# Stacking attention operands through a DRAM scratch in a fused attention and quantised-FFN kernel

## What is computed

```python
def attn(x, Wq, Wk, Wv, Wo):
    q = (x @ Wq).reshape(B, S, 16, 32).transpose(0, 2, 1, 3)
    k, v = (repeated 4 times over heads from (x @ Wk), (x @ Wv))
    scores = einsum('bhqd,bhkd->bhqk', q, k) / sqrt(32)
    out = einsum('bhqk,bhkd->bhqd', softmax(scores), v)
    return merge_heads(out) @ Wo
def ffn(x, weight, bias):
    w_q, w_scale = int8 rounding of weight by its row maximum / 127
    x_q, x_scale = int8 rounding of x by its token maximum / 127
    return (x_q @ w_q.T) * x_scale * w_scale + bias
x = layernorm(x + attn(x, ...)); x = layernorm(x + ffn(x, ...))
```

## Time and profile before

| | |
|---|---|
| median of 3 runs | 786.63 us (784.62 to 788.5) |
| profiled execution | 787.02 us, span 785.2 us |
| PE busy | 735.6 us (94%) |
| DVE, ACT, POOL busy | 615.2, 477.5, 596.8 us |
| chain that ended last, shares | PE 45%, POOL 16%, issue 15%, SP's queue 10% |
| of it SP's stacking issues, line 312 | 9% |

### The profile page before, as it was taken

One profiled execution on the slowest core, in us unless ns is written; L12 is line 12 of the kernel. 1 busy time (PEld: TensorE's weight loads), 2 busy tenths in 40 slices (PEclk: granted clock), 3 DMA queues, 4 the chain that ended last, 5 costly groups with the idle time before them and its releaser, 6 DMA issues.

```text
span 785.2 us, 12326 instructions
## 1 busy us (share of the span) xinstructions
PE 735.6 (94%) x3700; PEld 433.8 (55%) x3700; DVE 615.2 (78%) x1090; ACT 477.5 (61%) x872; POOL 596.8 (76%) x705
## 2 busy tenths in 40 slices
PE   8789989899899999999999999999999999999993
PEld 6455545566366654566446663666545664454451
DVE  3797888668987788886888789878888868888546
ACT  3165556556765576656666566656756666666735
POOL 4258858676997689885987779975998759898935
PEclk9799999999999999999999999999999999999997
DMA  7632223133231342223322332413422233022121
GB/s 213 175 95 55 56 58 96 52 91 101 67 111 46 101 100 91 69 72 91 95 80 71 95 101 63 122 41 94 108 84 68 76 93 102 28 56 67 51 47 54
DMA packets 56386, 65.57 MB, mean 84 GB/s; under 512 B 25665, under 2 KB 27713, under 8 KB 56321
## 3 DMA queue, kind: packets, MB, share of 16 engines
q1 hardware_dynamic: 55152, 61.91, 29.5%
q0 software_dynamic: 1168, 2.89, 1.5%
HBM read 20.71 MB, written 8.39 MB: 37 GB/s over the span
## 4 chain that ended last, share of the span: by engine, by line
PE 45%; POOL 16%; issue 15%; SPq 10%; ACT 4%; DVE 4%; DMA 3%; POOLq 3%; DVEq 0%; ACTq 0%
POOL prob_sum L1080 14%; PE front_bank L341 9%; SPq L312 9%; PE st_bank L416 8%; PE s_bank L385 7%; PE o_bank L433 7%; PE tail_bank L341 6%; PE z_bank L459 3%; POOLq L1089 2%; DVE row_max L865 2%; ACT probs L695 1%; PE front_bank L348 1%; PE tail_bank L529 1%; DMA xq_sb<-round_sb 1%; POOL x_tok L1098 1%
## 5 line engine op out<-in xcount | busy, mean ns | idle before, releaser
L865 DVE TENSOR_REDUCE row_max<-s_bank 128x1 f32<-128x512 f32 x496 | 329.1, 682 | 81.2 <-PE s_bank L385 78.4
L695 ACT ACTIVATE probs<-st_bank 128x512 f32<-128x512 f32 x512 | 290.4, 594 | 133.1 <-PE st_bank L416 114.5
L1080 POOL TENSOR_TENSOR prob_sum<-prob_sum,probs 128x512 f32<-128x512 f32 x248 | 310.6, 1285 | 8.1 <-ACT probs L695 8.1
L416 PE MATMUL st_bank<-q_stack,k_stack 98*128 98x512 f32 x512 | 224.6, 441 | 14.6 <-ACT probs L695 11.1
L385 PE MATMUL s_bank<-k_stack,q_stack 96*128 96x512 f32 x496 | 203.4, 412 | 8.3 <-DVE row_max L865 7.1
L1080 POOL TENSOR_TENSOR prob_sum<-probs 128x512 f32<-128x512 f32 x128 | 161.3, 1284 | 46.0 <-PE z_bank L459 23.9
L416 PEld LDWEIGHTS st_bank<-q_stack,k_stack 98*128 98x128 f32 x512 | 96.1, 188 | 104.8 <-ACT probs L695 55.0
L433 PE MATMUL o_bank<-probs,v_tok 128*32 128x512 f32 x1024 | 123.3, 598 | 0.1
L385 PEld LDWEIGHTS s_bank<-k_stack,q_stack 96*128 96x128 f32 x496 | 94.2, 190 | 40.2 <-DVE row_max L865 22.5
L1085 POOL TENSOR_TENSOR rs<-mv,small 128x1 f32<-128x1 f32 x64 | 12.2, 190 | 82.1 <-DVE mv L915 81.5
L433 PEld LDWEIGHTS o_bank<-probs,v_tok 128*32 128x32 f32 x1024 | 26.7, 109 | 59.4 <-issue 52.5
(11 more groups left out here) (199 smaller groups left out, 992.8 us busy)
## 6 DMA issues: line engine op xcount, KB each, us to landing
q_stack<-q_parts SPq DMA_DIRECT2D x348, 64.0 KB, 2.0
x_tok<-in_L_attn_x SPq DMA_DIRECT2D x36, 256.0 KB, 3.0
y_sb<-in_L_attn_x SPq DMA_DIRECT2D x28, 256.0 KB, 2.8
out<-z_sb SPq DMA_DIRECT2D x28, 256.0 KB, 2.1
k_stack<-k_parts SPq DMA_DIRECT2D x84, 64.0 KB, 2.0
probs<-in_L_attn_Wq SPq DMA_DIRECT2D x1, 1024.0 KB, 7.6
prob_sum<-in_L_attn_Wo POOLq DMA_DIRECT2D x4, 256.0 KB, 4.3
q_stack<-neg_max SPq DMA_DIRECT2D x64, 8.0 KB, 1.8
```

What stands on the lines that cost most here:

```text
L416: nc.tensor.matmul(st_bank[:, j % 2, :], k_stack[0:STACK_M, p, j, kt * P:(kt + 1) * P], q_stack[0:STACK_M, i, j, :], start=True, stop=True ...
L695: nc.scalar.activation(probs[:, kt, j, :], st_bank[:, j % 2, :], ACT.Exp, scale=SCALE).then_inc(exp_done, 1)
L865: nc.vector.tensor_reduce(row_max[:, i % 2, j * QT + qt:j * QT + qt + 1], s_bank[:, qt % 2, :], AX_X, ALU.max).then_inc(max_done, 1)
L1080: nc.gpsimd.tensor_tensor(prob_sum[:, j, :], first, probs[:, kt, j, :], ALU.add).then_inc(sum_done, 1)
```

## The change

A job is no longer copied by twelve DMAs inside the on-chip memory. `spill` writes its 128 by 2 by 512 parts in one DMA to a scratch in DRAM (`q_spill`, `k_spill`), and `fill` reads it back in three, one for each third of the stack, 32 partitions with four runs of 2 KB each. `fill` waits for the write's semaphore and for the last reader of the slot, and has its own place in SP's queue (`fill_sp`). ACT waits for the write alone before it reuses `q_parts` or `k_parts`. K and Q0 of batch 0 (SP and POOL) and Q2 of batch 0 (POOL) still go by twelve DMAs.

In the prologue Q1's second part follows the second pair of scores instead of the first, V's twelve passes stand behind pairs 2 to 7, two each, and VT behind the first part of Q2; `wkv_part(1)` on DVE moves ahead of Q0's split and `wq_part(2)` one pair forward. `diagonal_scales` moves from DVE to ACT. POOL's trial run of `pow` is preceded by a multiply and an add. All three tables have new places; of `MIDDLE` those of the front, SP and the second layer's first half are shown.

```diff
-FIRST_ORDER = (0, 1, 2, 3, K, Q0, Q1, Q2, V, VT, Q3)
+FIRST_ORDER = (0, 1, 2, 3, K, Q0, Q1, V, VT, Q2, Q3)
-FIRST_V_PE, FIRST_V_ACT, FIRST_VT = (0, 1, 2), 2, 3
+FIRST_V_AFTER = range(2, 8)
 MIDDLE = dict(
-    front_pe={Q3: (0, 1, 3, 4), 0: (5,), 1: (10,), 2: (13,), 3: (16,), K: (18, 22), Q0: (23, 24, 25, 27), V: (29, 30), VT: (33,), Q1: (36, 37), Q2: (44, 45)},
-    front_act={Q3: 3, 0: 5, 1: 10, 2: 13, 3: 16, K: 22, Q0: 27, V: 29, VT: 32, Q1: 38, Q2: 45},
-    front_dve={Q3: 4, 0: 6, 1: 11, 2: 15, 3: 16, K: 22, Q0: 27, Q1: 39, Q2: 45},
+    front_pe={Q3: (0, 1, 2), 0: (5,), 1: (10,), 2: (13,), 3: (17,), K: (18, 22), Q0: (23, 25, 26, 27), V: (29, 30), VT: (31,), Q1: (35, 36, 38), Q2: (44, 45)},
+    front_act={Q3: 4, 0: 6, 1: 10, 2: 12, 3: 16, K: 21, Q0: 26, V: 30, VT: 33, Q1: 37, Q2: 45},
+    front_dve={Q3: 4, 0: 6, 1: 11, 2: 14, 3: 16, K: 22, Q0: 27, Q1: 39, Q2: 47},
+    fill_sp={Q3: 10, K: 30, Q0: 28, Q1: 42, Q2: 48},
...
-    max_lo_dve=(11, 26, 45, 59),
+    max_lo_dve=(12, 27, 45, 59),
...
-    round_act=(21, 31, 39, 47),
-    unround_act=(22, 31, 43, 52),
-    turn_sp=(21, 29, 42, 49),
+    round_act=(20, 30, 41, 47),
+    unround_act=(22, 30, 42, 49),
+    turn_sp=(19, 27, 42, 46),
...
 FIRST = dict(
...
+    fill_sp={Q3: 15, K: 33, Q0: 28, Q1: 47, Q2: 53},
...
-DIAGONAL_DVE, SPREAD_SCALES = 44, 48
+DIAGONAL_ACT, SPREAD_SCALES = 44, 48
...
+        q_spill = nc.dram_tensor("q_spill", (GROUPS, P, 2, S), F32)
+        k_spill = nc.dram_tensor("k_spill", (2, P, 2, S), F32)
...
+        def spills_before(b, f):
+            return 0 if b == 0 and f == Q1 else 1 if b == 0 else 2 + (b - 1) * GROUPS + Q_JOB.index(f)
...
-                if n == 0:
+                if n == 1:
                     front_job(0, Q1, first_bank[Q1], None, FIRST_Q1_PASSES[1])
+                if n in FIRST_V_AFTER:
+                    if n == FIRST_V_AFTER[0]:
+                        pe.wait_ge(front_lo, SPLIT_AT[Q1] + 1)
+                        pe.wait_ge(wkv_lo_done, 2)
+                    front_job(0, V, first_bank[V], None, share(n - FIRST_V_AFTER[0], len(FIRST_V_AFTER)))
...
             front_job(0, Q2, first_bank[Q2], None, FIRST_Q2_PASSES[0])
+            pe.wait_ge(front_hi, place(0, V) + 1)
+            front_job(0, VT, first_bank[VT], first_parts[V])
...
             def front_in_turn(b, p, f):
                 if f in Q_JOB:
-                    n = Q_JOB.index(f)
-                    wait(act, q_stacked[n - 1], (b + (n > 0)) * STACKED)
-                if f == K:
-                    wait(act, k_stacked, b * STACKED)
+                    if b == 0:
+                        act.wait_ge(q_stacked[0], STACKED)
+                    act.wait_ge(q_spilled, spills_before(b, f) * 16)
                 if f == V:
-                    act.wait_ge(k_stacked, (b + 1) * STACKED)
+                    act.wait_ge(k_spilled, b * 16)
...
+            def diagonal_scales():
+                act.wait_ge(w_t_done, KC - 1)
+                act.wait_ge(w_stat_done, 2 * KC)
+                act.wait_ge(ident_set, 2)
+                for o in range(KC):
+                    nc.scalar.mul(y_sb[:, o * P:(o + 1) * P], ident[:], w_stat[:, 1, o:o + 1]).then_inc(w_diag_done, 1)
...
             max_hi(0, 0)
+            first_front(VT)
             first_front(Q2)
...
-            def diagonal_scales():
-                dve.wait_ge(w_t_done, KC - 1)
-                for o in range(KC):
-                    nc.vector.tensor_scalar(y_sb[:, o * P:(o + 1) * P], ident[:], w_stat[:, 1, o:o + 1], None,
-                                            ALU.mult).then_inc(w_diag_done, 1)
...
             wq_part(1)
+            wkv_part(1)
             first_front(Q0)
             for n in range(FIRST_PAIRS):
                 first_maxima(n)
                 if n == 1:
                     first_front(Q1)
-                if n == 4:
-                    wkv_part(1)
-                if n == 6:
+                if n == 5:
                     wq_part(2)
...
-            nc.gpsimd.tensor_tensor(rs1[:, 0, 3:4], small[:, 1:2], small[:, 0:1], ALU.pow)
+            nc.gpsimd.tensor_tensor(rs1[:, 0, 3:4], small[:, 1:2], small[:, 2:3], ALU.mult)
+            nc.gpsimd.tensor_tensor(rs1[:, 0, 0:1], small[:, 1:2], small[:, 1:2], ALU.add)
+            pool.drain()
+            nc.gpsimd.tensor_tensor(rs1[:, 0, 1:2], rs1[:, 0, 0:1], small[:, 0:1], ALU.pow)
...
-            def stack_front(b, p, f, parts):
+            def spill(b, p, f, parts):
                 sp.wait_ge(front_lo, b * SPLITS + SPLIT_AT[f] + 1)
-                hi, lo = parts[:, 0, :], parts[:, 1, :]
                 if f == K:
-                    stack_heads(sp, range(NKV), k_stack[:, p, :, :], (hi, lo, hi), k_stacked)
+                    wait(sp, k_stacked, (b - 1) * STACKED)
+                    sp.dma_start(k_spill[p], parts[:]).then_inc(k_spilled, 16)
                 else:
                     i = Q_JOB.index(f)
+                    wait(sp, q_stacked[i], b * STACKED)
+                    sp.dma_start(q_spill[i], parts[:]).then_inc(q_spilled, 16)
+            def fill(b, p, f):
+                if f == K:
+                    sp.wait_ge(k_spilled, b * 16)
+                    dst, src, order, done = k_stack[:, p, :, :], k_spill[p], (0, 1, 0), k_stacked
+                else:
+                    i = Q_JOB.index(f)
+                    sp.wait_ge(q_spilled, (spills_before(b, f) + 1) * 16)
                     wait(sp, st_done, (b - 1) * UNITS + (i + 1) * QT * NKV)
-                    stack_heads(sp, range(NKV), q_stack[:, i, :, :], (hi, hi, lo), q_stacked[i])
+                    dst, src, order, done = q_stack[:, i, :, :], q_spill[i], (0, 0, 1), q_stacked[i]
+                for r, part in enumerate(order):
+                    sp.dma_start(dst[r * HEAD:(r + 1) * HEAD, :, :].bitcast(F32),
+                                 src[:, part, :].rearrange("(j p) s -> p j s", j=NKV)).then_inc(done, 16)
...
-                            stack_front(b if f == Q3 else b + 1, p if f == Q3 else 1 - p, f, k_parts if f == K else q_parts)
+                            spill(b if f == Q3 else b + 1, p if f == Q3 else 1 - p, f, k_parts if f == K else q_parts)
+                    for f, unit in plan["fill_sp"].items():
+                        if u == unit and (front or f == Q3):
+                            fill(b if f == Q3 else b + 1, p if f == Q3 else 1 - p, f)
```

More of the change, by code:

```diff
@@ L75 @@
-    ffn_pe=(27, 36, 48, 56),
+    max_hi_act=(10, 25, 45, 56),
+    max_lo_dve=(12, 27, 45, 59),
+    o_hi_act=(10, 25, 46, 57),
+    o_lo_dve=(11, 31, 48, 63),
+    wo_pe=((9, 11, 14), (19, 20, 21, 22), (33, 34), (40, 41, 42, 43)),
+    load_sp=(5, 12, 27, 37),
+    res1_dve=(14, 22, 35, 43),
+    stats1_dve=(16, 23, 35, 43),
+    rstd1_pool=(22, 29, 37, 45),
+    norm1_act=(19, 29, 37, 47),
+    maxx_dve=(19, 28, 39, 47),
+    round_act=(20, 30, 41, 47),
+    unround_act=(22, 30, 42, 49),
+    turn_sp=(19, 27, 42, 46),
@@ L76 @@
+    bias_pool=(24, 35, 43, 55),
+    load_x_sp=(2, 3, 4, 4),
+    ffn_pe=(28, 36, 48, 56),
     rescale_dve=(29, 36, 49, 57),
[L77 removed]
+    res2_dve=(30, 38, 52, 60),
     stats2_dve=(33, 38, 52, 61),
[L79 to L80 removed]
+    rstd2_pool=(36, 38, 56, 63),
+    norm2_act=(36, 40, 54, 63))
 FIRST = dict(
[L82 removed]
@@ new lines @@
+    front_act={Q3: 5, 0: 8, 1: 9, 2: 12, 3: 14, K: 21, Q0: 24, V: 30, VT: 34, Q1: 41, Q2: 50},
+    front_dve={Q3: 6, 0: 8, 1: 10, 2: 12, 3: 14, K: 22, Q0: 25, Q1: 42, Q2: 52},
+    fill_sp={Q3: 15, K: 33, Q0: 28, Q1: 47, Q2: 53},
+    sums_pe=(12, 23, 35, 53),
+    inv_act=(15, 24, 37, 53),
+    correct_dve=(0, 23, 39, 55),
+    scale_dve=(19, 24, 41, 55),
+    norm_dve=(0, 29, 43, 63),
+    max_pe=(12, 25, 42, 57),
+    max_hi_act=(14, 26, 42, 56),
+    max_lo_dve=(13, 26, 42, 58),
+    o_hi_act=(10, 29, 49, 62),
@@ L96 @@
+    o_lo_dve=(4, 30, 50, 63),
+    load_x_sp=(0, 0, 0, 1))
 LAST = dict(
-    front_pe={Q3: (0, 1, 3, 5, 9)},
+    front_pe={Q3: (0, 1, 2, 4, 5, 9)},
     front_act={Q3: 9},
[L99 to L124, removed]
@@ L125 @@
-    stats2_dve=(29, 42, 49, 61),
-    rstd2_pool=(32, 47, 57, 62),
-    norm2_act=(35, 46, 59, 63))
+    front_dve={Q3: 10},
+    fill_sp={Q3: 20},
+    sums_pe=(6, 21, 37, 55),
+    inv_act=(5, 23, 37, 55),
+    correct_dve=(6, 23, 37, 54),
+    scale_dve=(7, 23, 40, 58),
+    norm_dve=(9, 23, 40, 59),
+    max_pe=(10, 28, 43, 63),
+    max_hi_act=(10, 28, 44, 62),
+    max_lo_dve=(12, 28, 43, 61),
+    o_hi_act=(10, 32, 42, 59),
+    o_lo_dve=(10, 32, 42, 60),
+    wo_pe=((10, 11, 12, 14), (18, 23, 25), (31, 33, 35), (40, 44)),
@@ new lines @@
+    load_sp=(3, 19, 23, 38),
+    res1_dve=(14, 25, 35, 42),
+    stats1_dve=(14, 27, 35, 43),
+    rstd1_pool=(18, 30, 38, 47),
+    norm1_act=(17, 29, 38, 53),
+    maxx_dve=(19, 30, 42, 44),
+    round_act=(20, 31, 44, 53),
+    unround_act=(24, 32, 47, 57),
+    turn_sp=(22, 34, 49, 55),
+    bias_pool=(21, 37, 52, 61),
+    load_x_sp=(30, 39, 57, 58),
+    ffn_pe=(28, 37, 53, 59),
```

(12 more changed lines are left out.)

61 lines of the change are left out of this document (13 added, 48 removed).

## The result

| kernel | median us | range us, runs | ratio to before, 95% interval |
|---|---|---|---|
| before | 786.85 | 784.62 to 788.50, 4 | 1 |
| after | 817.09 | 815.58 to 818.52, 4 | 1.0363 (1.0325 to 1.0401) |

The change makes the kernel 30 us slower; the forecast was 10.7 us faster. The profiled execution of after took 818.52 us, its span 816.7. PE's busy time grew to 756.0 us with the same matmuls; its mean granted clock fell from 0.985 to 0.966 of full speed.

The account below looks back on a forecast made before the run. PE was taken as the bound, busy 88.60 of 91 us in a middle batch. Gains of 1.5 + 2.7 (prologue), 2.3 (scales) and 4.2 (SP's queue) made 10.7 us, from 787.02 to 776.3; range 767 to 786.

Parts of the forecast that it names:

- Stacking by scratch: Middle batches: 444 issues become 148, job latency about as before, SP free between write and fill; 4.2 us, bounds 0 and 8.
- Rival A: Middle batches: fills come late for the next batch at unit 40, margin nothing to minus 2 us; slower, 798; chance 0.10.
- SP's relief: Middle batches: SP's queue, freed of issues, evens batches out to the shortest, 90.57 us; gain 4.2 us.
- Rival B: Middle batches: SP's relief is worth nothing, only prologue and scales count; 780.5 us; chance 0.17.
- Prologue: Batch 0: first unit starts 1.5 us earlier, and 2.7 us more is won from 37.2 to 61.7 us.
- item (3): Prologue: scores waiting for Q1's stack come 1.6 us earlier, its last fill landing at 30.4.
- item (4): Prologue: V's twelve passes move between the pairs, covered by PE's 2.4 us idle; VT ahead of the first unit costs 0.6.
- item (5): Prologue: a busier PE may keep its clock; at most 2 us at stake, 0.5 taken.
- items (1) and (2): Prologue: Q1's second part and `wkv_part(1)` move, so the transpose of the maxima comes 1.4 us earlier.
- items (6) and (7): Units from 37.2 to 61.7 us: PE loses V's work, row maxima wait less behind Q3; together 2.7 us, bounds 1 and 3.3.
- Scales: Near 100 us: diagonal scales leave DVE for ACT, so PE's wait goes; gain 2.3 us, bounds 1.3 and 2.3.
- Rivals C (785) and D (769.7): C: prologue's gain is lost again to DVE, chance 0.13; D: pow's stall goes, freed queue gives 8.6 us, chance 0.15.

Follow-up runs that it names:

- e7: The kernel before with the scratch alone, write and three fills back to back where the twelve DMAs stood; 785.84 us, ratio 0.9957.
- e8: The kernel after without the store of tile 0 in batches 0 to 6; 792.75 us, ratio 1.0053.
- e9: The kernel before with the scratch in place of the twelve DMAs and the diagonal scales on ACT; 781.53 us, ratio 0.9921.
- e6: The kernel after with K's fill at place 25, SP's second tile transpose and third residual load at 29, in middle batches; 786.37 us, ratio 0.9962.
- e2: The kernel after with tile 0's store issued by ACT instead of SP; 811.92 us, ratio 1.0271.
- e3: The kernel after with V and VT of batch 0 back in units 0 to 3; 810.37 us, ratio 1.0264.
- e5: The kernel after with K's fill at place 25 and V and VT of batch 0 back in units 0 to 3; 790.60 us, ratio 1.0016.
- e10: As e6, the kernel after with fills ahead of the second tile transpose, plus V and VT of batch 0 back in units 0 to 3; 787.74 us, ratio 0.9991.
- e4: The kernel before with only the diagonal scales moved from DVE to ACT; 788.32 us, ratio 0.9988.

## Why the prediction was wrong, point by point

**The step that failed** is the last sentence of "Stacking by scratch": "the traffic is covered", by a mean share of the DMA engines (0.32 of a batch, 0.43 after). The mean held: by the windows of after from 395 to 468 and from 468 to 495 it is 0.30 and 0.54, 0.36 together. But it isn't spread. The share is 1.0 for 7 us, and those are the 7 us in which a store must land that a single buffer waits for. The latency of a job was worked out "alone", and alone it is right (in e7 a job takes 8.4 us by the median, from the write's issue to the landing of the last fill, where 8.4 was worked out). It was never asked what is issued behind the six fills and who waits for that.

**Rival A** had the place and the lateness, and its chance was too low. The fills were put at 0 to 2 us late for unit 40; the trace shows 1.4 on the mean and 1.9 at most (six waits, 8.3). e8 shows what this alone costs: some 11 us, about the 10.7 from which A was to decide (its 7 x 1.5 is 10.5, and six batches wait, not seven). It would have made the kernel 4 us slower than before, not 30. A priced the consumer of the fills and not the bystander on the same DMA engines, nor the clock that PE loses after an idle stretch.

**SP's relief, 4.2 us:** right in size where the places are kept: 3.4 in e7 by the timed runs, though its trace shows 1.2, and five batches 4.1 us shorter and nearly even in e9. That it is SP's queue and not ACT's earlier reuse of the parts isn't shown. Rival B (worth nothing) falls by the times of e7 and e9. With the new places it is worth nothing: e6 has no jump and no gain from event 7 on.

**Prologue, 1.5 and 2.7 us:** wrong. SP did what was worked out (Q1's write issued at 23.03, its fills at 26.65; forecast 23.0 and 26.5). But in item (3) the landing was taken at 2.0 us behind the last issue, 30.4; the last fill landed 4.6 behind it, at 32.06, so nothing of the 1.6 was won. In e8, where PE gets there in time, the timeline of PE has the same scores as late as the earlier trace rows:

```profile
32.17 0.74 PE L396 MATMUL s_bank<-k_stack,q_stack 96*128 96x512 f32 x2 [1.06 <-DMA q_stack<-q_spill]
```

The term of item (4) that PE's 2.4 us of idle time cover V's passes failed too. In the profiled execution PE ran the pairs at half clock, as PE's timeline and the windows show:

```profile
23.80 1.65 PE L409 MATMUL s_bank<-o_hi,q_parts 32*128 32x512 f32 x6
25.37 0.80 PE L352 MATMUL tail_bank<-x_lo,wkv_hi 128*128 128x512 f32 x1
25.97 0.63 PE L352 MATMUL tail_bank<-x_hi,wkv_lo 128*128 128x512 f32 x1
26.52 1.65 PE L409 MATMUL st_bank<-o_hi,q_parts 32*128 32x512 f32 x6
```

```profile
20.00:30.00 10.00, 9.23 (x36) 4.52 (x34) 6.59 (x7) 0.73 (x2) 3.23 (x7) 0.66 0.76 210
30.00:40.00 10.00, 9.76 (x31) 6.01 (x28) 4.03 (x6) 1.09 (x3) 0.00 (x0) 0.50 0.27 66
```

A pair takes 2.72 us, where DVE's maxima set 1.23; the first maxima stand at 35.02 instead of 30.89. The same code in e2's profiled execution, in the same windows, kept the clock:

```profile
20.00:30.00 10.00, 9.23 (x48) 4.60 (x48) 8.54 (x9) 1.03 (x2) 3.55 (x8) 1.00 0.74 201
30.00:40.00 10.00, 6.62 (x29) 4.71 (x28) 6.58 (x11) 4.04 (x8) 1.32 (x3) 1.00 0.67 200
```

There the first maxima stand at 30.89, as before, not earlier; with V back they stand at 29.72 in e3, 29.92 in e5 and 28.98 in e10, so about the 1.4 us of items (1) and (2) came, and V's passes took them. By event 7, e8, whose clock was 1.00 until 30 us, is 3.7 us ahead of before and after itself 0.1 behind. So item (5), the clock, can go either way, for some 4 us. At event 4, ahead of the gain of the scales, e2 is level with before (+0.05) and e8 1.3 us behind, and e9, with the old prologue, is level too (+0.07): the new order wins nothing even where the clock is kept. Of the 2.7 of items (6) and (7), after wins 0.2 and e2 1.1 between events 1 and 3, e8 nothing. In the timed medians V's place can't be seen at all (e10 against e6).

**Scales, 2.3 us:** right by the traces (e4's timed runs can't tell it from nothing). ACT's four passes take 1.27 us in the timeline, where DVE's took 4.45:

```profile
104.23 1.27 ACT L731 ACTIVATE y_sb<-ident,x_scale 128x128 f32<-128x128 f32 x4
```

The events gain 2.7 us there in after (the difference goes from +5.1 at event 4 to +2.4 at event 5) and 2.6 in e9. **POOL, 0:** right; the stall ahead of the first pow of batch 1 is what it was in the earlier trace rows:

```profile
153.40 0.56 POOL L1094 TENSOR_TENSOR rs<-rs,small 128x1 f32<-128x1 f32 x1 [2.54 <-issue]
```

Rivals C (785) and D (769.7) had neither the burst nor the lateness in them.

What stays open: the 6 us of the jumps that neither PE's idle time nor the clock accounts for; why the same prologue keeps its clock in one execution and not in another; and whether a second `z_sb` would do as well as moving the fills. That wasn't tried.

## What to carry to other kernels

A DMA that is cheap alone has to be priced with what is issued right behind it: six fills of 256 KB held the DMA engines full for 7 us, and the store behind them, with a single buffer waiting for its landing, cost some 19 of the 30 us in the middle batches (e8). Freeing a queue lets transfers stack up in bursts, so look for the first thing behind a burst that an in-order engine waits for; a mean DMA share of 0.36 says nothing of it. And run the parts of a bundled change apart: the scratch and the scales in their old places were 6 us faster than before, while the new places and the new prologue won nothing.

## What the runs showed of the hardware that was not expected

- The fills, each into 32 partitions, moved at 220 to 255 GB/s with the DMA engines' share at 1.0 (a store and a load of 256 KB each among them), where three loads into 128 partitions moved 348. The Trainium skill has in *SBUF — State Buffer*, "Door 1: the DMA port swizzle", that partitions 0 to 31 and 32 to 63 lie on the same 8 of 16 ports. By that, an estimate, four of the six fills share one half of them: 1 MB at 218 GB/s is 4.8 us, and the measured landing of 6.8, counted from the issue of K's fills, lies 2.0 above it, a bare copy's latency. No run here separates the ports from other limits.
- A store on ACT's queue, with nothing of that queue ahead of it, landed in 7.0 us (2.2 for the others of the same run, by SP).
- Idle time of 2.5 to 4.4 us on PE, in pieces of up to 1.9, was followed in three of six batches by some 7 us at half clock, in a fourth by 3.5, in two by none (worked out from the mean clock of the six windows). With the same code in the prologue, PE busy 9.23 of 10 us, the granted clock was 0.66 in one execution and 1.00 in another.
